# A chain of eight layers on one core: other instruction kinds on VectorE, closing rows in one instruction, routing in nine items, one maximum per causal head

## The chip, the core and the metric

The kernel runs on one core of a Trainium2 chip, as one program. The metric is the device time of one execution in microseconds. The kernel before takes 3289.19 us, the median of three runs (3284.95 to 3290.69).

## The reference

The input x is 16 x 256 x 256 (16 items of 256 tokens, 256 channels), with a context of the same shape and a mask of 16 x 256. Eight layers follow one another, each a residual addition:

```python
x = x + xattn0(layernorm(x), ctx)          # 16 heads, relu on q, k, v
x = x + ffn0(layernorm(x))                 # 8 experts, the best one
x = x + xattn1(layernorm(x), ctx, mask)    # 16 heads, own norms, masked
x = x + ffn1(layernorm(x))                 # 4 experts with low-rank parts
x = x + xattn2(layernorm(x), ctx)          # 16 heads, biases
x = x + block(layernorm(x))                # x + causal attention(norm(x)), then x + moe(norm(x))
x = x + xattn3(layernorm(x), ctx)          # 8 heads of 64
x = x + fp8_linear(layernorm(x))           # x and weight rounded to fp8, rows @ weight.T
```

The mixture in `block` keeps two of eight experts for each token: the logits are compared, the two largest chosen, and their outputs weighted. `fp8_linear` scales by 448 / max|x|, rounds to float8 and multiplies back.

## The kernel before, in words

The activations stay in SBUF as 32 tiles of 128 tokens. `attention()` is built for each attention layer; the unit of its work is one item of 256 tokens. It is software-pipelined: a list written out by hand (`slots()`, line 375 on, and `plan()`, lines 457 to 510) gives each period 16 slots. A period is one item in the steady state. In each slot TensorE does a head's scores and a head's product, and VectorE, ScalarE and GpSimd run the same list, each taking the entries that are its own. `SHIFT` says which item a step of a period is for: "l" is six items behind. Two attentions (the one that uses the context, a2, and the causal one, a3) run in one block, without a barrier; tiles of both are called a2... in the trace. Every step waits for semaphores counted by `Signal.at`.

What the change touches:

- **Biases and variances.** VBB (line 1154) is V's bias, spread over 128 rows: a tensor_scalar of ones by a column, twice, on VectorE. VE (lines 1284 to 1288) is the variance plus epsilon, made on VectorE; GpSimd raises it to the power -0.5 (line 734), with a constant tile `neghalf` of 8 columns.
- **GpSimd at the head of an attention.** It makes the normalised rows of item 0, then `keys()` and `others()` (lines 720 to 726) clear KS, QS, NM and VA; in the masked attention the mask rows MKF and MROW follow (lines 821, 822), which K needs. Then it issues the DMAs that move Q (line 598) and goes on to the next item. K is moved by SyncE's queue.
- **The maximum of a causal head** (line 1214). Scores of 256 queries against keys lie in one bank: 128 columns for the first 128 queries (which see only the first 128 keys), 256 for the second 128. Two VectorE reduces make the two maxima. TensorE then transposes the maxima of all heads (`maxT`).
- **The router** (class `Router`, line 72). Items are routed in five groups, `GROUPS = [(0, 4), (4, 8), (8, 12), (12, 14), (14, 16)]`. Items 0 to 13 have their logits made inside the causal attention, items 14 and 15 in the block of the routed experts. For a group VectorE ranks the experts of each token (`choose`, line 219), copies the running ranks that TensorE sums (`ranks`, `ranked`), works out which slots of 256 rows belong to which expert (`runs`, line 259) and each token's places (`places`, line 284). These are four items of the plan, in slots 1, 3, 5 and 7 of the period after the group's last logits. GpSimd then scatters each item's normalised rows into `slots` with four indirect DMAs (`scatter`, line 304), one item per period (`late`, line 317).
- **The entry of the routed experts** (`routed`, line 1939). Behind the barrier VectorE does the statistics of the last two items, their logits, the last group's routing, the table of slots, and the lower halves of the weights in 16 pieces (`low`, line 2131; ScalarE's `high`, line 2085, makes the upper ones). The pieces pass through a ring of four buffers, f2WF: piece j is loaded when low(j-4) is done. TensorE begins when the last low is done and the rows of the first slot are loaded, which waits for all scatters.
- **The quantised layer** (`quantised_linear`, line 2220). For each of eight units VectorE rounds (lines 2293 to 2301; the last is a subtraction of two SBUF tiles into Q), and writes the rows of an earlier unit from PSUM with scale and bias in four pieces of 256 columns (line 2315); GpSimd adds X and the result leaves (line 2259).

## Time and profile before

| | |
|---|---|
| median of three runs | 3289.19 us |
| the profiled execution | 3291.92 us, its span 3290.2 us |
| mean granted TensorE clock | 0.928 of full speed |
| TensorE busy | 2804.8 us (85%) |
| VectorE busy | 1978.9 us (60%) |
| ScalarE busy | 1666.2 us (51%) |
| GpSimd busy | 1142.0 us (35%) |
| causal attention with routing, from its first output to its last | 2045.1 to 2342.6 us |
| entry of the routed experts | 2343 to 2412 us |

Times are of one execution taken by the hardware profiler. A row of a timeline reads: start, duration, engine, line, operation, output and inputs with the number of instructions, and in brackets how long the engine had stood idle and what ended that. PE is TensorE, DVE VectorE, ACT ScalarE, POOL GpSimd, SP SyncE; the letter q behind a name means its queue of DMA issues. A view by windows gives the busy time of each engine in a stretch, the granted clock (PEclk) and the DMA traffic. Several instructions that overlap in one row, as x2 or x4, share one duration from the first start to the last end.

### The profile page before, as it was taken

Reading aid. Unit: us, or ns where it says so; the run is one execution under the profiler, and the core shown is the slowest. Engines: PE = TensorE matmul, PEld = TensorE weight load, DVE = VectorE, ACT = ScalarE, POOL = GpSimd, SP = SyncE. Lnnn points to the kernel's source line nnn. Section 1 sums busy time; section 2 is a strip of 40 time slices with the busy share of each in tenths; the row PEclk is TensorE's granted clock in tenths of the full one; section 3 lists DMA queues with packets and bytes.
Section 4 is the critical chain, followed back from the end, with each engine's and each line's share of the span. In section 5 each row is a group of like instructions: output and inputs, shape, how many; then the busy total and the mean of one; then the engine's idle time right before and its main releaser. Section 6 shows DMA issues by size and latency. Waiting matters only on the chain. (4 is left out here: it accounts for less than half of the span.)

```text
span 3290.2 us, 69997 instructions
## 1 busy us (share of the span) xinstructions
PE 2804.8 (85%) x26085; PEld 1887.7 (57%) x26085; DVE 1978.9 (60%) x4610; ACT 1666.2 (51%) x3073; POOL 1142.0 (35%) x1192
## 2 busy tenths in 40 slices
PE   4998685888789999999969999988469959999993
PEld 2554453555346666666645556666258846666672
DVE  4887556888555344443358887788554344555547
ACT  2778332777544444444437776666455523333332
POOL 6653008777000000000043334465410074555423
PEclk8999896999889999999979999999789978999995
DMA  3332002221214000000011211111243243332301
GB/s 116 79 75 56 14 8 88 67 67 64 45 55 151 1 1 1 1 1 1 1 60 59 75 48 48 43 56 63 80 145 92 88 114 71 79 87 61 76 21 51
DMA packets 164743, 189.87 MB, mean 58 GB/s; under 512 B 25968, under 2 KB 136832, under 8 KB 164256
## 3 DMA queue, kind: packets, MB, share of 16 engines
q1 hardware_dynamic: 147520, 143.44, 14.8%
q0 software_dynamic: 16896, 41.97, 4.9%
q8 instruction: 218, 3.57, 0.5%
q14 instruction: 109, 0.89, 0.1%
HBM read 67.09 MB, written 41.42 MB: 33 GB/s over the span
## 5 line engine op out<-in xcount | busy, mean ns | idle before, releaser
L1920 DVE TENSOR_TENSOR f1H<-f1HF,f1H 128x512 bf16<-128x512 f32 x256 | 176.6, 692 | 398.2 <-ACT f1H L1760 398.2
L1693 PE MATMUL ps<-f1xT,f1w 128*128 128x512 bf16 x1536 | 378.3, 383 | 6.1 <-ACT f1H L1760 6.1
L1715 PE MATMUL ps<-f1w,f1H 128*128 128x256 bf16 x3072 | 378.1, 273 | 0.0
L1715 PEld LDWEIGHTS ps<-f1w,f1H 128*128 128x128 bf16 x3072 | 301.4, 98 | 90.2 <-issue 1.1
L1757 ACT ACTIVATE f1HF<-ps 128x512 f32<-128x512 f32 x256 | 152.8, 597 | 333.9 <-PE ps L1693 333.8
L1075 ACT ACTIVATE a2PT<-ps 128x512 f32<-128x512 f32 (+1 forms) x512 | 260.1, 542 | 81.5 <-PE ps L892 58.1
L1693 PEld LDWEIGHTS ps<-f1xT,f1w 128*128 128x128 bf16 x1536 | 148.2, 98 | 150.8 <-issue 16.7
L869 PE MATMUL ps<-a2KS,a2QS 49*128 49x256 bf16 (+1 forms) x1024 | 173.7, 263 | 56.1 <-DVE a2NM L1217 19.7
L734 POOL TENSOR_TENSOR a2RS<-a2VE,neghalf 128x4 f32<-128x4 f32 x32 | 32.7, 1021 | 539.7 <-DVE a2VE L1288 539.7
L1603 POOL TENSOR_TENSOR f1RS<-f1VE,neghalf 128x4 f32<-128x4 f32 x8 | 8.1, 1011 | 574.6 <-DVE f1VE L1903 574.6
L1217 DVE TENSOR_REDUCE a1NM<-ps 128x2 f32<-128x512 f32 x256 | 165.7, 686 | 38.6 <-PE ps L869 37.3
L1217 DVE TENSOR_REDUCE a0NM<-ps 128x2 f32<-128x512 f32 x256 | 165.2, 685 | 35.1 <-PE ps L869 34.7
L1217 DVE TENSOR_REDUCE a2NM<-ps 128x2 f32<-128x512 f32 x256 | 165.6, 685 | 25.1 <-PE ps L869 23.1
L1075 ACT ACTIVATE a4PT<-ps 128x512 f32<-128x512 f32 x128 | 76.0, 597 | 193.7 <-PE ps L881 193.7
L881 PE MATMUL ps<-a2QS,a2KS 51*128 51x256 bf16 (+1 forms) x1024 | 171.0, 262 | 0.2 <-ACT a2PT L1075 0.2
L1214 DVE TENSOR_REDUCE a2NM<-ps 128x1 f32<-128x128 f32 (+1 forms) x512 | 150.2, 349 | 28.9 <-PE ps L892 26.9
L1075 ACT ACTIVATE a1PT<-ps 128x512 f32<-128x512 f32 x256 | 143.0, 595 | 26.6 <-PE ps L881 24.7
L809 POOL DMA_INDIRECT Y<-results,IX x64 | 63.3, 990 | 260.7 <-DMA results<-f2OB 243.7
L869 PEld LDWEIGHTS ps<-a2KS,a2QS 49*128 49x128 bf16 x1024 | 66.8, 94 | 148.4 <-DVE a2NM L1217 50.6
L1760 ACT ACTIVATE f1H<-ps 128x512 bf16<-128x512 f32 x256 | 151.7, 593 | 0.0
L1075 ACT ACTIVATE a0PT<-ps 128x512 f32<-128x512 f32 x256 | 141.5, 593 | 15.5 <-PE ps L881 12.0
L869 PE MATMUL ps<-a4KS,a4QS 128*128 128x256 bf16 (+1 forms) x512 | 126.6, 283 | 16.6 <-issue 8.6
(533 smaller groups left out, 7043.0 us busy)
## 6 DMA issues: line engine op xcount, KB each, us to landing
a2KS<-a2KH SPq DMA_DIRECT2D x192, 64.0 KB
a2QS<-a2QH SPq DMA_DIRECT2D x192, 64.0 KB
a4KS<-a4KH SPq DMA_DIRECT2D x96, 128.0 KB
a4QS<-a4QH POOLq DMA_DIRECT2D x96, 128.0 KB, 4.2
slots<-zeros SPq DMA_DIRECT2D x1, 9984.0 KB, 31.9
f2XG<-slots SPq DMA_DIRECT2D x39, 256.0 KB, 3.0
results<-f2OB SPq DMA_DIRECT2D x39, 256.0 KB, 2.1
f1WF<-in_f_w SPq DMA_DIRECT2D x32, 256.0 KB, 2.7
```

The lines of the kernel that those rows point to most:

```text
L734: nc.gpsimd.tensor_tensor(RS[:, h], VE[:, h], g["neghalf"][:, 0:4], ALU.pow).then_inc(S["rstd_ready"].sem, 1)
L809: nc.gpsimd.indirect_dma_start(GB[:, t % 4, k, :], None, g["results"][:, :], bass.IndirectOffsetOnAxis(ap=g["IX"][:, k, t:t + 1], axis=0)) ...
L869: m = nc.tensor.matmul(bank[:, at:at + keys], QS[r0:r1, u % RING, ch, gi, t * P:t * P + P], KS[r0:r1, u % RING, ch, gi, 0:keys], start=(ch ...
L881: m = nc.tensor.matmul(bank[:, at:at + SEQ - q0], KS[r0:r1, u % RING, ch, gi, t * P:t * P + P], QS[r0:r1, u % RING, ch, gi, q0:SEQ], start ...
L1075: nc.scalar.activation(PT[:, ic % 8, 0:n_], ps[:, 2 + (uc * NH + ic) % 3, 0:n_], ACT.Exp, scale=scale).then_inc(S["p_ready"].sem, 1)
L1214: s_ = nc.vector.tensor_reduce(NM[:, u % 2, t, col:col + 1], bank[:, lo:hi], AX.X, MAX, negate=True)
L1217: s_ = nc.vector.tensor_reduce(NM[:, u % 2, :, col:col + 1], bank.rearrange("p (t k) -> p t k", t=2), AX.X, MAX, negate=True)
L1693: m = nc.tensor.matmul(ps[:, (u * NCH + i) % 2, :], w1[:, x, kt, i * P:i * P + P], xT[:, half, y, kt, :], start=(j == 0), stop=(j == len(t ...
L1715: m = nc.tensor.matmul(out, H[:, (u * NCH + i) % HR, x, t * P:t * P + P], w2[:, y, i, :], start=first, stop=(f == YC - 1 and j == 2 and no ...
L1757: nc.scalar.activation(HF[:, (u * NCH + i) % 2, :], ps[:, (u * NCH + i) % 2, :], cfg["gelu"], **bias).then_inc(S["h_full"].sem, 1)
L1760: nc.scalar.activation(H[:, (u * NCH + i) % HR, 0, :], ps[:, (u * NCH + i) % 2, :], cfg["gelu"], **bias).then_inc(S["h_hi"].sem, 1)
L1920: nc.vector.tensor_tensor(H[:, (u * NCH + i) % HR, 1, :], HF[:, (u * NCH + i) % 2, :], H[:, (u * NCH + i) % HR, 0, :], SUB).then_inc(S["h_ ...
```

## The change

It has six parts.

1. VBB, VE, and the last subtraction of Q and WQ in the quantised layer become scalar_tensor_tensor; epsilon comes from columns 4 to 7 of `neghalf`, which VectorE sets at the start. In the masked attention `keys()` and `others()` run behind the mask rows.
2. The closing rows of a unit of the quantised layer are one scalar_tensor_tensor of 128x1024 instead of four of 128x256.
3. A causal head has one reduce over three blocks of 128 columns; behind the last head of an item a minimum (maxima are stored negated) joins the second and the third, and TensorE's transposes wait for that (`m_full`).
4. Routing is nine items, in slots 1 to 9; the group (8, 12) has its scatters two items to a period, behind slot 10.
5. The group (12, 14) is routed in the block of the routed experts (`PLACED = 3`), beside the statistics of the last two items, and all its scatters are issued there.
6. In that block lows 0 to 5 are spread between the routing steps, the table comes behind low 5, and ScalarE's highs and copies alternate.

```diff
+PLACED = 3
 def late(u):
-    a, b = [q for q in GROUPS if q[0] <= u < q[1]][0]
-    return BATCH + b - 1 + 6 + u - a
+    n, (a, b) = [(k, q) for k, q in enumerate(GROUPS) if q[0] <= u < q[1]][0]
+    return BATCH + b - 1 + 6 + (u - a) // (2 if n + 1 == PLACED else 1) if n < PLACED else None
...
-            put(1, "r_choose", "l", 0)
-            put(3, "r_rank", "l", 0)
-            put(5, "r_runs", "l", 0)
-            put(7, "r_places", "l", 0)
+            for k, n in enumerate(("r_compare", "r_select", "r_count", "r_rank", "r_need", "r_first", "r_jump", "r_place",
+                                   "r_index")):
+                put(1 + k, n, "l", 0)
...
-                        if r == "l" and v + 1 != GROUPS[n][1]:
+                        if r == "l" and (v + 1 != GROUPS[n][1] or n >= PLACED):
...
-                if router and k == 9:
+                if router and k == 10:
                     made += [("r_scatter", v, 0, None, None) for v in range(INSIDE) if late(v) == period]
...
-        NM = sb("NM", [P, 2, 2, P], F32)
+        NM = sb("NM", [P, 2, 3 if any(q.causal for q in stages) else 2, P], F32)
...
-                        nc.gpsimd.memset(g[n][:], v).then_inc(built.sem, 1)
+                        nc.gpsimd.memset(g[n][:, 0:4] if n == "neghalf" else g[n][:], v).then_inc(built.sem, 1)
...
-                        if u == 0 and not gather:
+                        if u == 0 and not gather and not mask:
                             keys()
                             others()
...
                                            ALU.is_equal, MUL).then_inc(S["mask_row"].sem, 1)
+                        if u == 0:
+                            keys()
+                            others()
...
-                        pe.wait_ge(S["s_max"].sem, S["s_max"].at(u, NH))
+                        if stage(u).causal:
+                            pe.wait_ge(S["m_full"].sem, S["m_full"].at(u % BATCH, 1))
+                        else:
+                            pe.wait_ge(S["s_max"].sem, S["s_max"].at(u, NH))
...
-                        v = nc.vector.tensor_scalar(VBB[:, kt, :], g["onesf"][:, 0:P], VB[:, kt:kt + 1], None, MUL)
+                        v = nc.vector.scalar_tensor_tensor(VBB[:, kt, :], g["onesf"][:, 0:P], VB[:, kt:kt + 1],
+                                                           g["onesf"][:, 0:P], MUL, MUL)
...
                         if stage(u).causal:
-                            for t, (lo, hi) in enumerate(((0, P), (P, P + SEQ))):
-                                s_ = nc.vector.tensor_reduce(NM[:, u % 2, t, col:col + 1], bank[:, lo:hi],
-                                                             AX.X, MAX, negate=True)
+                            s_ = nc.vector.tensor_reduce(NM[:, u % 2, :, col:col + 1],
+                                                         bank[:, 0:3 * P].rearrange("p (b k) -> p b k", b=3),
+                                                         AX.X, MAX, negate=True)
...
+                        if stage(u).causal and i == NH - 1:
+
+                            dve.wait_ge(S["s_max"].sem, S["s_max"].at(u, NH))
+                            nc.vector.tensor_tensor(NM[:, u % 2, 1, 0:NH], NM[:, u % 2, 1, 0:NH], NM[:, u % 2, 2, 0:NH], MIN
+                                                    ).then_inc(S["m_full"].sem, 1)
...
-                        a1, b1 = (1.0 + EPS, EPS * EPS) if stage(u).ln == 2 else (1.0, EPS)
-                        s_ = nc.vector.tensor_scalar(VE[:, h, 0:2], v, a1, b1, MUL, ADD)
+                        a1, b1 = (1.0 + EPS, 6) if stage(u).ln == 2 else (1.0, 4)
+                        s_ = nc.vector.scalar_tensor_tensor(VE[:, h, 0:2], v, a1, g["neghalf"][:, b1:b1 + 2], MUL, ADD)
...
+                router.ranks(pe, PLACED, ps[:, 4, :])
                 for u in LATE:
                     router.transposes(pe, u, ps[:, u % 2, :])
...
-                for j in range(4):
-                    high(j)
-                for u in LATE:
-                    router.copied(act, u, ps[:, u % 2, :])
+                high(0)
+                high(1)
+                router.copied(act, INSIDE, ps[:, INSIDE % 2, :])
+                high(2)
+                high(3)
+                router.copied(act, INSIDE + 1, ps[:, (INSIDE + 1) % 2, :])
...
-                for u in LATE:
-                    router.stats(dve, u)
-                    router.negate(dve, u)
-                for u in LATE:
-                    router.kept(dve, u, ps[:, 2 + u % 2, :])
-                router.choose(dve, LAST)
+                router.stats(dve, INSIDE)
+                router.compare(dve, PLACED)
+                router.negate(dve, INSIDE)
+                router.stats(dve, INSIDE + 1)
+                router.select(dve, PLACED)
+                router.count(dve, PLACED)
+                router.negate(dve, INSIDE + 1)
+                router.ranked(dve, PLACED, ps[:, 4, :])
+                router.need(dve, PLACED)
+                router.first(dve, PLACED)
+                router.jump(dve, PLACED)
+                router.place(dve, PLACED)
+                router.index(dve, PLACED)
                 low(0)
+                router.kept(dve, INSIDE, ps[:, 2 + INSIDE % 2, :])
+                low(1)
+                router.kept(dve, INSIDE + 1, ps[:, 2 + (INSIDE + 1) % 2, :])
+                router.compare(dve, LAST)
+                router.select(dve, LAST)
+                router.count(dve, LAST)
+                low(2)
                 router.ranked(dve, LAST, ps[:, 5, :])
-                router.runs(dve, LAST)
-                router.places(dve, LAST)
+                router.need(dve, LAST)
+                router.first(dve, LAST)
+                router.jump(dve, LAST)
+                low(3)
+                router.place(dve, LAST)
+                router.index(dve, LAST)
+                low(4)
+                low(5)
                 table()
-                for j in range(1, len(PIECES)):
+                for j in range(6, len(PIECES)):
                     low(j)
...
-                    nc.vector.tensor_tensor(Q[:], t1, t2, SUB).then_inc(S["q_ready"].sem, 1)
+                    nc.vector.scalar_tensor_tensor(Q[:], t1, 1.0, t2, MUL, SUB).then_inc(S["q_ready"].sem, 1)
...
-                    for t in range(UT):
-                        acc = ps[:, 2 * (c % 2) + t // 2, (t % 2) * D:(t % 2) * D + D]
-                        v = nc.vector.scalar_tensor_tensor(OB[:, c % 2, t * D:t * D + D], acc, IS[:, 2:3], q8["BI"][:], MUL, ADD)
-                    v.then_inc(S["q_ob"].sem, 1)
+                    acc = ps[:, 2 * (c % 2):2 * (c % 2) + 2, :].rearrange("p b (t d) -> p (b t) d", d=D)
+                    bias = q8["BI"][:].rearrange("p (one d) -> p one d", one=1).to_broadcast([P, UT, D])
+                    nc.vector.scalar_tensor_tensor(OB[:, c % 2].rearrange("p (t d) -> p t d", d=D), acc, IS[:, 2:3], bias,
+                                                   MUL, ADD).then_inc(S["q_ob"].sem, 1)
...
+                nc.vector.memset(g["neghalf"][:, 4:6], EPS)
+                nc.vector.memset(g["neghalf"][:, 6:8], EPS * EPS)
```

The new functions `compare`, `select` and `count` hold the instructions of `choose`, `need`, `first` and `jump` those of `runs`, `place` and `index` those of `places`; no instruction is added or taken away by that.

## Rows read from the trace of the kernel before

**Rows 1.** Windows: us; PE, PEld, DVE, ACT, POOL busy; PEclk; DMA share; GB/s.

```profile
523.90:557.00 33.10, 15.22 (x96) 8.02 (x96) 16.98 (x44) 4.25 (x7) 31.78 (x36) 0.67 0.30 73
2144.57:2171.34 26.77, 20.98 (x294) 14.30 (x290) 24.00 (x86) 14.44 (x29) 15.92 (x14) 0.94 0.15 51
2171.34:2191.07 19.73, 18.89 (x288) 13.60 (x284) 15.48 (x57) 14.03 (x29) 14.06 (x14) 1.00 0.22 71
2230.60:2257.10 26.50, 19.99 (x298) 13.78 (x295) 24.04 (x87) 14.44 (x29) 15.90 (x14) 1.00 0.15 51
2343.00:2412.00 69.00, 4.03 (x53) 2.90 (x53) 36.79 (x97) 21.31 (x22) 33.17 (x31) 0.50 0.51 178
```

**Rows 2.** timeline of VectorE at the heads of three attentions: start us, us, instruction.

```profile
505.67 12.23 DVE L1154 TENSOR_SCALAR a1VBB<-onesf,a1VB 128x128 f32<-128x128 f32 x2
...
1667.00 0.88 DVE L1171 SCALAR_TENSOR_TENSOR a2wq<-a2PT,a2VEC,a2wq 128x256 bf16<-128x256 f32 x2 [6.41 <-ACT a2wq L1056]
...
1671.72 5.38 DVE L1154 TENSOR_SCALAR a2VBB<-onesf,a2VB 128x128 f32<-128x128 f32 x2
...
2672.74 4.72 DVE L1284 TENSOR_SCALAR a4VE<-a4MV 128x2 f32<-128x2 f32 x1
```

**Rows 3.** timeline of GpSimd at the heads of the first two of these.

```profile
506.95 3.51 POOL L721 MEMSET a1KS<- 128x4096 f32 x1
...
519.07 1.06 POOL L822 TENSOR_SCALAR a1MROW<-a1MKI 8x256 bf16<-8x256 int32 x1
524.03 3.14 POOL L598 DMA_DIRECT2D a1QS<-a1QH  x6 [3.90 <-issue]
...
1666.08 3.51 POOL L721 MEMSET a2KS<- 128x4096 f32 x1
```

**Rows 4.** quantised layer: timelines of VectorE and GpSimd, and line 2301 by itself.

```profile
3239.65 3.02 DVE L2301 TENSOR_TENSOR q8Q<-q8T 128x1024 bf16<-128x1024 f32 x1
3242.60 1.65 DVE L2315 SCALAR_TENSOR_TENSOR q8OB<-ps,q8IS,q8BI 128x256 bf16<-128x256 f32 x4
...
3238.50 3.09 POOL L2259 TENSOR_TENSOR q8OUT<-X,q8OB 128x1024 f32<-128x1024 f32 x1 [20.36 <-DVE q8T L2296]
...
L2301 DVE TENSOR_TENSOR q8Q<-q8T x8: 1225/3024/3025, 3227.6 to 3275.7; 128x1024 bf16<-128x1024 f32 x8
```

**Rows 5.** timeline of VectorE and GpSimd in a routing period of the causal attention.

```profile
2320.80 1.13 DVE L276 SCALAR_TENSOR_TENSOR f2FREE<-f2T 128x8 f32<-128x8 f32 x1
...
2320.74 1.17 POOL L177 TENSOR_TENSOR f2XS<-a2WF,f2XS 128x512 bf16<-128x512 f32 x1
```

**Rows 6.** causal maxima, line 1214, in one unit by form, and in a row of four.

```profile
L1214 DVE TENSOR_REDUCE a2NM<-ps 128x1 f32<-128x256 f32 x16 | 6.6, 414 | 0.0
L1214 DVE TENSOR_REDUCE a2NM<-ps 128x1 f32<-128x128 f32 x16 | 4.5, 283 | 0.8 <-PE ps L892 0.8
...
2154.49 1.14 DVE L1214 TENSOR_REDUCE a2NM<-ps 128x1 f32<-128x128 f32 x4
```

**Rows 7.** TensorE's waits in five periods (2045 to 2144), then in the first routing period.

```profile
PE ps L869 <- DVE a2NM L1214: 3.6, 6, 1.6
...
PE ps L869 <- DVE a2NM L1214: 3.2, 3, 1.8
PE ps L242 <- DVE f2SEL L233: 1.7, 1, 1.7
```

**Rows 8.** timeline of GpSimd around the entry of the routed experts.

```profile
2325.18 1.05 POOL L313 DMA_INDIRECT slots<-f2XS,IX  x1 [3.27 <-DVE IX L302]
...
2360.06 0.14 POOL L2009 IOTA f2JI<- 128x1 int32 x1 [4.25 <-POOLq L601]
```

**Rows 9.** timeline of VectorE and TensorE in the entry of the routed experts.

```profile
2377.02 1.28 DVE L2136 SCALAR_TENSOR_TENSOR f2w<-f2WF,f2GA,f2w 128x1024 bf16<-128x1024 f32 x1
...
2390.93 1.28 DVE L2136 SCALAR_TENSOR_TENSOR f2w<-f2WF,f2GA,f2w 128x1024 bf16<-128x1024 f32 x1 [1.38 <-ACT f2w L2089]
...
2412.29 1.86 PE L2042 MATMUL ps<-identb,f2XG 128*128 128x128 bf16 x16 [27.75 <-issue]
```

112 lines of the change are left out of this document (69 added, 43 removed).

## The prediction

> **What bounds the kernel now.** I went from the time by stage to the two engines' timelines in the stages that the edits touch. TensorE carries most stages, but not everywhere: in the causal attention a plain period of 19.73 us holds 18.89 us of TensorE work and 15.48 of VectorE, so TensorE paces it, with 0.84 us left over. The two periods that route a whole group of four items last 26.77 and 26.50 us, with VectorE busy for 24.00 and 24.04 and TensorE for 20.98 and 19.99: there VectorE paces [rows 1]. From 2343 to 2412 us TensorE works 4.03 of 69 us [rows 1]: that is the routed experts' entry, a chain of routing, scatters and weight preparation. At the head of the masked attention (523.9 to 557 us) it works 15.22 of 33.10 us, with GpSimd busy for 31.78; there, and in the closing quantised layer, the waits of VectorE and GpSimd count at full price.
>
> **1. Another instruction kind.** VectorE's tensor_scalar of 128x128 into VBB, twice, lasts 12.23 us in the masked attention and 5.38 in the next one, and the tiny VE in the gathering attention 4.72; each ends with a series of GpSimd memsets [rows 2, 3]. Its scalar_tensor_tensor of two SBUF inputs at 1667.00 takes 0.88 for the pair under the memset that runs from 1666.08 to 1669.59 [rows 2, 3]: that kind is not held by a memset. So VBB ends at some 507.3 (a GpSimd operation that reads runs until 507.0, then 0.3), and the held time goes. What is late next: GpSimd's own queue. Before, its keys' and others' memsets run from 506.95 to 517.92 and the mask rows to 520.13, then it waits 3.90 for the Q move at 524.03, for VectorE's late Q and K [rows 3]. After, the mask rows come first (to 509.2), K and Q are ready under the memsets, which end at 520.3, and the Q move follows at once. From that move to 557 GpSimd is busy for 31.78 of 33.10 us [rows 1], so it takes along what it gains: **-3.8**, of at most 6.3 that the K side gets (the mask rows come 11 earlier, but K's move must wait for the memset of KS); 0 if the K side or the mask load becomes last. In the next attention VBB's release brings K's lower half forward by about **-1.3** (0 to -4). In the gathering attention the power that follows VE stands on GpSimd behind the very memsets that hold VE [rows 2], and GpSimd's gathers and Q move come after it, so the freed time has no taker: **0** (to -2). The two new memsets of the constants, 0.1 each, run before anything waits: 0.
>
> **The quantised layer's subtraction** is the doubtful one. As tensor_tensor it takes 1.23 us at its shortest and 3.02 in the median; the one at 3239.65 stands beside GpSimd's addition, which reads SBUF from 3238.50 to 3241.59, and six of the eight are held so [rows 4]. As scalar_tensor_tensor it has the same two inputs in SBUF. The nearest row of that kind beside a GpSimd operation that reads is the one at 2320.80: 1.13 instead of 0.16, until GpSimd's addition of 1.17 ends [rows 5]. So it is held alike: **0**; the other bound is that it isn't held, 6 x 1.79 = -10.8. The Trainium skill ("SBUF — State Buffer", Who interferes with whom) has a rule that speaks against this edit: a VectorE instruction with two SBUF inputs contends with a GpSimd instruction that reads SBUF, and not with one that only writes. By that rule the edit on Q brings nothing and that on VBB all; rows 5 and the pair at 1667.00 agree.
>
> **2. Closing rows.** Four pieces take 1.65 us, one 128x1024 operation 1.23 [rows 4]: 0.42 less, at seven of eight units on VectorE's chain: **-3.0**. The bounds are 0 (GpSimd, which starts on the rows, may move its hold along) and -4. The quantised weights' single operation, 0.7 us, keeps its length: 0.
>
> **3. One maximum per causal head.** Before, 16 reduces of 128x128 (0.28) and 16 of 128x256 (0.41), 11.1 us a unit. They overlap: two pairs last 1.14, a pair 0.57 [rows 6]. From 0.28 for 128 and 0.41 for 256 elements, 384 take 0.55, spaced 0.48: 16 x 0.09 = 1.4 less, against which the minimum of 128x16 and its own wait add 0.3 to 0.6 at the end of the unit: VectorE gets 0.8 to 1.1 back. TensorE's transposes of the maxima now wait for that minimum; it is behind the last reduce by 0.3 and they are a slot away: 0. The wider memset of NM adds 0.3 in the head of the stage, beside VectorE's work: 0. TensorE waits 3.6 us on these reduces in the first five periods [rows 7], 0.7 in each. I take 0.35 for each of eleven plain periods: **-4**, between 0 and -8 (nearly all of the 0.84).
>
> **4. Nine routing items, two scatters to a period.** A routing period needs 24.0 us of VectorE, 23.2 with part 3, and lasts 26.6: 2.5 us of it are holes where four long items stand in front of a reduce for which TensorE waits. With pieces of 1 to 2 us in nine slots I halve the holes: 24.8, **-1.8** twice, and -1.2 for the group of half the size: -4.8 (0 to -9; nothing if the links between items, now with TensorE's ranks in slot 4 and waits in more places, make new holes). The two scatter items of a period issue eight indirect DMAs instead of four, 10.1 us of GpSimd's queue at 1.265 each. Behind them stand the power, and through it VectorE's negate and ScalarE's normalising of the last items; they come some 4 us later, in periods whose own work ends on TensorE, and GpSimd's chain below counts them.
>
> **5. The entry of the routed experts.** Before: the last attention's output at 2342.6, the group (12, 14) routed behind it until 2350.8, four scatters until 2355.8, then 4.25 us to the next block's first GpSimd instruction at T0 = 2360.06; low(0) at T0 + 17, the last low a little before TensorE, TensorE at T0 + 52.2, after 27.75 us without work [rows 8, 9]. After: that group is routed inside the block beside the statistics, the power and the split, which leave VectorE idle for most of the first 12 us of the block. T0 is set by GpSimd: from the index of group (8, 12) at about 2325, two items' scatters (10.1), power, normalising and split (4), two items' again (10.1), and 4.25 behind them, T0 = 2353.9: -6. low(0), which frees the ring of four weight buffers, comes at T0 + 11.5 behind the routing of group 3, and the lows follow the weights' loads as before: another -5.8. Together **-11.8**. Bounds: -4 (only the block starts sooner, by less; all 16 scatters of the last four items stand in the block as before, and the lows are paced by loads) and -16.
>
> Sum: -3.8 - 1.3 - 3.0 - 4.0 - 4.8 - 11.8 = **-28.7**. The profiled execution took 3291.92 us, 2.7 above the median of the runs; 3291.92 - 28.7 = 3263.2, and on the median 3289.19 - 28.7 = **3260.5 us**.
>
> **The rivals.** (A) The subtraction isn't held in the new kind: 10.8 more, 3249.7. For it: under a memset the kind matters, as the pair at 1667.00 beside VBB shows, so it might beside a reader too; against it, the one row of that kind beside a reader [rows 5]. Chance 0.17. (B) The causal stage stays with TensorE, whose 18.89 of 19.73 leaves little, and the entry is paced by the weights' loads: parts 3 and 4 give 2 and part 5 gives 6: -16, 3273. For it: at 2390.93 a low waits for ScalarE's high of the same piece, as most of those behind it [rows 9]. Chance 0.22. (C) The instruction kind does nothing for VBB, since two operands make it wait as before: the 5.1 of part 1 go, 3265.6; the pair at 1667.00 is against it. Chance 0.08. (D) Slower: the clock. In the first routing period, where TensorE waits 3.2 us on the maxima and 1.7 on the selection [rows 7], the granted clock is 0.94 and its work 20.98 us instead of 19.99: the drop cost 1.0 [rows 1]. If nine items, with their waits in every slot of VectorE, spread such holes over the period, TensorE could stay at the lower of its two levels: its 19 us would be 38. From two whole periods this decides: -28.7 + 38 = +9, 3298. Against it: the second routing period has its holes at 1.00. Chance 0.03. The forecast has 0.50.
>
> **The numbers.** A measurement of this kernel tells about 0.2%, 6.6 us, from no change. All cases but D lie below 3282.6; B with low ends in every part could come near it. The range reaches from A with some gain less than full (3247) to a little below B (3274). Faster 0.93, same 0.04, slower 0.03.
>
> **What would show it.** VBB pairs of under 1.5 us; the first Q move of the masked attention at about 520.3; the subtraction still 3.02 in six of eight; closing rows as one of about 1.2; plain causal periods of 19.4 and routing periods near 25; T0 six us sooner against the last attention's output, and 46 instead of 52 us from T0 to TensorE's first turn. I am wrong if the subtraction falls to 1.2, if routing periods stay at 26, or if the lows wait for loads so that T0 + 52 stands.

## The result and the profile after

The changed kernel takes 3273.39 us, median of six runs (3270.53 to 3276.84), where the kernel before took 3289.94 beside it. The ratio is 0.9951, with a 95% interval from 0.9935 to 0.9967: 16 us faster (11 to 21), more than the 0.2% that a measurement tells from no change. The profiled execution took 3275.65 us, its span is 3273.9 us, at a mean clock of 0.928. Another chip gave 0.9954 (0.9940 to 0.9967). One execution of a later kernel (the old order of memsets) took 11164.78 us at a granted clock of 0.239 and is left out of its ratio.

The forecast was 28.7 us. To see where the rest went, I cut both traces at VectorE's write of each unit's output (line 1360 before, 1404 after) and at the landmarks of the prediction. All figures are of the two profiled executions:

| stretch | forecast | before | after | difference |
|---|---|---|---|---|
| masked attention: first power to first Q move | -3.8 | 28.44 | 24.39 | -4.05 |
| next attention: first power to first scores | -1.3 | 26.88 | 25.25 | -1.63 |
| causal stage: twelve plain periods | -4 | 231.89 | 228.24 | -3.65 |
| causal stage: two full routing periods | -3.6 | 53.27 | 57.82 | **+4.55** |
| third last output to T0 (third routing, tail, block change) | -7.2 | 48.19 | 43.52 | -4.67 |
| T0 to TensorE's first expert turn | -5.8 | 52.23 | 46.64 | -5.59 |
| quantised layer: last output to the end | -3.0 | 77.33 | 74.69 | -2.64 |

Five of the seven are within 1 us of what was said. Two aren't: the routing periods are 8.2 us off, with the wrong sign, and the stretch to T0 is 2.5 off. That is nearly the whole difference of 12 us between forecast and measurement. The entry of the routed experts and the block change hold parts 5 and 6 of the change together; no run takes them apart.

What these rows leave out (layers that the change doesn't touch, and the gathering attention) moves by several us between executions of one kernel: from the first expert turn to the first output of the gathering attention the changed kernel took 370.44 us in one profile and 363.68 in another, and its executions on the second chip reach from 3261.31 to 3280.18 us. So below I compare stretches, and use whole times for the verdicts only. Periods of the causal stage repeat to 0.2 us, but where TensorE's clock falls they can be 1 to 1.6 us apart.

Windows over the first routing period, a plain one, the second and the third routing period, and the entry, after; they answer to [rows 1], with the same columns:

```profile
2136.91:2165.72 28.81, 21.09 (x295) 14.63 (x293) 23.20 (x71) 14.34 (x29) 15.61 (x14) 0.94 0.14 48
2165.72:2185.25 19.53, 18.83 (x285) 13.57 (x283) 14.66 (x41) 14.07 (x29) 14.06 (x14) 1.00 0.22 71
2224.34:2253.35 29.01, 21.69 (x295) 14.75 (x293) 23.17 (x72) 14.33 (x29) 15.53 (x14) 0.88 0.14 48
2307.68:2330.68 23.00, 18.55 (x185) 11.04 (x184) 12.66 (x45) 11.54 (x25) 9.07 (x10) 0.70 0.12 41
2343.80:2398.00 54.20, 4.22 (x55) 3.09 (x56) 37.95 (x97) 21.19 (x22) 29.97 (x27) 0.54 0.64 217
```

VectorE has less to do than before (23.20 instead of 24.00 us), and yet the period is 2 us longer. The clock is lower in the second and the third: TensorE's same work takes 21.69 instead of 19.99 us, and in the third 18.55 instead of 14.46 (the clock was 0.90 there before). In the first it is 0.94 as before, with 21.09 us of work for 20.98.

The timeline of VectorE and GpSimd at the heads of the two attentions, after, to [rows 2, 3]:

```profile
508.05 1.62 DVE L1182 SCALAR_TENSOR_TENSOR a1VBB<-onesf,a1VB 128x128 f32<-128x128 f32 x2
514.58 0.88 DVE L1343 SCALAR_TENSOR_TENSOR a1KF<-ps,a1bk,a1MKF 128x256 f32<-128x256 f32 x2 [4.91 <-PE ps L884]
...
1668.12 0.61 DVE L1182 SCALAR_TENSOR_TENSOR a2VBB<-onesf,a2VB 128x128 f32<-128x128 f32 x2
...
1666.25 3.51 POOL L746 MEMSET a2QS<- 128x4096 f32 x1
...
510.76 1.06 POOL L844 TENSOR_SCALAR a1MROW<-a1MKI 8x256 bf16<-8x256 int32 x1
519.14 3.50 POOL L748 MEMSET a1VA<- 128x4096 f32 x1
522.60 3.14 POOL L620 DMA_DIRECT2D a1QS<-a1QH  x6
```

VBB is short (its second piece stands beside GpSimd's subtraction, so the pair takes 1.62 and not 0.61 us), the mask rows end at 511.8, and the Q move starts with no idle time, right behind the memset. In the span's own time it is 1.4 us sooner; from the first power, at 498.21 here and at 495.59 before, it is 4.05 sooner. The first output of this attention comes 99.85 us behind the power instead of 103.32, so 3.5 us of it are still there then. In the next attention the first scores come 1.63 us sooner and the first output 0.64 (83.03 instead of 83.67).

The quantised layer, after, to [rows 4]:

```profile
3225.64 3.02 DVE L2369 SCALAR_TENSOR_TENSOR q8Q<-q8T 128x1024 bf16<-128x1024 f32 x1
3228.59 1.27 DVE L2383 SCALAR_TENSOR_TENSOR q8OB<-ps,q8IS,q8BI 128x1024 bf16<-128x1024 f32 x1
...
3224.49 3.09 POOL L2327 TENSOR_TENSOR q8OUT<-X,q8OB 128x1024 f32<-128x1024 f32 x1 [19.99 <-DVE q8T L2364]
...
L2369 DVE SCALAR_TENSOR_TENSOR q8Q<-q8T x8: 1224/3024/3026, 3214.0 to 3259.8; 128x1024 bf16<-128x1024 f32 x8
```

The subtraction is as long as it was, in six of eight units. The closing rows are one operation of 1.27 us.

The selection of the first full group, in the timelines of VectorE and TensorE, and TensorE's waits in that period, after, to [rows 7]:

```profile
2138.49 0.67 DVE L227 TENSOR_TENSOR a2WF<-f2G 128x512 f32<-128x512 f32 x1
2145.83 0.64 DVE L242 TENSOR_SCALAR f2SEL<-f2RK 128x64 bf16<-128x64 f32 x1
...
2146.62 0.21 PE L252 MATMUL ps<-f2SEL,prior 128*128 128x64 bf16 x1 [5.11 <-DVE f2SEL L242]
...
PE ps L252 <- DVE f2SEL L242: 5.1, 1, 5.1
PE ps L894 <- DVE a2NM L1252: 2.2, 3, 1.0
```

This is what the prediction did not have in it. VectorE begins to compare at 2138.49 and has the selection at 2146.47, because it takes the three items in three slots, with two reduces, K's lower half, a unit's product and its statistics between them: 8 us, where one item took 4.1. TensorE is at its rank product in slot 4 by 2141.5 and waits 5.11 us. Before, the item was in one piece in slot 1, the ranks in slot 3, and the wait was 1.7.

The entry of the routed experts, after, to [rows 8, 9]:

```profile
2351.20 0.14 POOL L2055 IOTA f2JI<- 128x1 int32 x1 [4.25 <-POOLq L623]
...
2343.80 0.69 DVE L1404 TENSOR_TENSOR Y<-ps,Y 128x512 f32<-128x512 f32 x1 [1.53 <-PE ps L884]
2363.14 1.28 DVE L2184 SCALAR_TENSOR_TENSOR f2w<-f2WF,f2GA,f2w 128x1024 bf16<-128x1024 f32 x1
...
2397.83 1.86 PE L2088 MATMUL ps<-identb,f2XG 128*128 128x128 bf16 x16 [18.69 <-issue]
```

T0 is 2351.20, low(0) at T0 + 11.9, TensorE at T0 + 46.6, as forecast (11.5 and 46). T0 comes 7.40 us behind the last output instead of 17.51.

What sets T0 is in GpSimd's timeline, after; the first and the last row each open a series of eight indirect DMAs, four for each of two items:

```profile
2321.24 1.05 POOL L336 DMA_INDIRECT slots<-f2XS,IX  x1 [7.00 <-DVE IX L325]
...
2335.03 0.61 POOL L176 CAST f2XS<-a2WF 128x512 bf16<-128x512 f32 x1 [3.14 <-ACT a2WF L166]
...
2337.04 1.05 POOL L336 DMA_INDIRECT slots<-f2XS,IX  x1 [0.17 <-issue]
```

The first scatter starts 13.56 us behind the third last output (13.31 before). Eight scatters take 9.9 us, the power, the wait for ScalarE's normalising and the split 5.9, eight more scatters 9.9, and then come the 4.25 us: 43.5 in all.

And the clock around the second wait and behind the third, in windows of the changed kernel, columns as in [rows 1]:

```profile
2229.00:2234.30 5.30, 0.24 (x7) 0.28 (x8) 5.13 (x13) 1.46 (x3) 5.15 (x6) 0.78 0.16 52
2234.30:2237.00 2.70, 2.70 (x25) 1.88 (x23) 0.87 (x3) 0.49 (x1) 1.27 (x2) 0.50 0.19 55
2237.00:2240.00 3.00, 3.00 (x39) 1.64 (x38) 1.20 (x5) 1.31 (x3) 0.00 (x0) 0.70 0.00 0
...
2318.00:2323.00 5.00, 5.00 (x44) 2.86 (x40) 2.54 (x14) 3.21 (x8) 1.46 (x2) 0.50 0.03 12
2323.00:2328.00 5.00, 5.00 (x40) 2.89 (x40) 1.21 (x3) 2.64 (x5) 3.78 (x5) 0.55 0.29 103
```

TensorE works 0.24 of 5.3 us while it waits, and the clock falls to half within that wait; then it runs at 1.2 GHz for 2.7 us and for a part of the next three. The third wait, of 4.4 us, ends at 2315.2, and TensorE stays at 1.2 GHz until about 2327.5, though it works all the time from 2318 on.

### The profile page after: what moved, and what is told of

Same layout as the page of the kernel before. It is cut to its first block and busy times, and to the rows that moved or that the text cites. A ratio compares the mean times of both kernels' runs of the same rounds, so it can differ in the third digit from the quotient of the medians.

```text
span 3273.9 us, 69748 instructions
## 1 busy us (share of the span) xinstructions
PE 2807.5 (86%) x26085; PEld 1890.0 (58%) x26085; DVE 1943.4 (59%) x4348; ACT 1666.0 (51%) x3073; POOL 1142.5 (35%) x1192
## 5 line engine op out<-in xcount | busy, mean ns | idle before, releaser
L1252 DVE TENSOR_REDUCE a2NM<-ps 128x3 f32<-128x384 f32 x256 | 134.5, 553 | 32.8 <-PE ps L917 30.0
```

What stands on the lines that cost most here:

```text
L1252: s_ = nc.vector.tensor_reduce(NM[:, u % 2, :, col:col + 1], bank[:, 0:3 * P].rearrange("p (b k) -> p b k", b=3), AX.X, MAX, negate=True)
```

## The experiments

All edits are made to the changed kernel, the last ones on top of the ranks in slot 6. Ratios are to the kernel before on the same chip. The four kernels with two reduces, the old kinds, the old order and the later addition have ratios whose intervals overlap that of the changed kernel (0.9935 to 0.9967): what is said of them rests on stretches of one profile each.

### Four items again; and nine, with the ranks two slots later

```diff
-            for k, n in enumerate(("r_compare", "r_select", "r_count", "r_rank", "r_need", "r_first", "r_jump", "r_place",
-                                   "r_index")):
-                put(1 + k, n, "l", 0)
+            for k, n in ((1, "r_compare"), (1, "r_select"), (1, "r_count"), (3, "r_rank"), (5, "r_need"), (5, "r_first"),
+                         (5, "r_jump"), (7, "r_place"), (7, "r_index")):
+                put(k, n, "l", 0)
```

> The changed kernel with the routing's nine functions called in four items again, in slots 1, 3, 5 and 7, all else as changed. Theory W (TensorE's rank product in slot 4 waits for a selection that now lies behind three slots of VectorE's work, 5.1 and 4.4 us instead of 1.7 and 2.7, and its clock falls after the wait): the two full routing periods go from 28.8 and 29.0 us to 25.5 to 26.5, the third from 23.0 to 17 to 18.5, the wait on the selection falls under 2.8 us, and the kernel to about 3264 us (3261 to 3268). Rival X (the one maximum and its minimum make the stage slow): periods stay at 28.5 to 29, the time at 3273. Rival Y (two scatters a period delay the tail): the full periods recover, the third stays at 22 to 23, the time is about 3268.5.

Ratio 0.9917 (0.9902 to 0.9931), 3270.82 us. Windows over the two full routing periods and the last period, then the wait on the selection in the second:

```profile
2139.50:2166.97 27.47, 22.54 (x295) 15.46 (x293) 23.71 (x71) 14.32 (x29) 16.05 (x14) 0.88 0.15 50
2225.60:2253.98 28.38, 23.62 (x295) 16.26 (x293) 23.71 (x71) 14.49 (x29) 15.97 (x14) 0.82 0.14 48
2326.47:2344.63 18.16, 11.71 (x120) 7.29 (x119) 2.90 (x8) 6.74 (x14) 13.45 (x15) 0.73 0.23 80
...
PE ps L252 <- DVE f2SEL L242: 1.7, 1, 1.7
```

The wait on the selection is back at 1.7, and the full periods are 27.47 and 28.38 us: shorter than with nine items in slots 1 to 9, but outside what I had said, and longer than before the change (26.78 and 26.49). The clock did that: TensorE is busy for 22.54 and 23.62 us with work that takes 20 at full clock. These periods differ from those of before mainly in the one maximum per head, and the waits are no longer than they were. Whether the one maximum lowers the clock or this execution fell further by chance, one profile can't tell; by the two executions named below chance is good for 1 to 1.6 us of a period.

The third period is 18.09 us, from 23.00, but the last one went from 13.12 to 18.16, so their sum is the same. That is theory Y (two scatters a period delay the tail) in another place: see the split scatters below.

```diff
+            for k, n in ((1, "r_compare"), (2, "r_select"), (3, "r_count"), (6, "r_rank"), (7, "r_need"), (8, "r_first"),
+                         (9, "r_jump"), (10, "r_place"), (11, "r_index")):
+                put(k, n, "l", 0)
...
-                if router and k == 10:
+                if router and k == 12:
```

> The changed kernel with nine items, but the ranks two slots later: compare, select and count in slots 1 to 3, ranks in slot 6, the rest in 7 to 11, scatters behind slot 12. Theory W: TensorE waits under 0.7 us for the selection, the full routing periods take 23.5 to 25.5 us, the third 16.5 to 18, and the kernel 3260 us (3257 to 3266). If it is the number of items itself, with a wait in every slot, that costs (rival Z), the full periods stay above 27.5 us and the time at 3270 or more. By Y the third period stays at 22 to 23.

Ratio 0.9917 (0.9901 to 0.9932), 3268.43 us. Windows over the two full routing periods:

```profile
2139.77:2164.22 24.45, 19.83 (x295) 13.74 (x293) 22.68 (x71) 14.64 (x29) 13.89 (x12) 1.00 0.14 46
2223.22:2249.21 25.99, 21.52 (x296) 14.74 (x295) 22.74 (x71) 14.86 (x29) 14.31 (x13) 0.93 0.14 46
```

They take 24.45 and 25.99 us, 4.36 and 3.02 less than in the changed kernel, with the same number of items. The second is a little above what I had said, and so is the third (18.45 us), which keeps a wait of 3.2 us on the selection. From the two full periods that wait is gone; 4.1 us of waits on the maxima remain, in five pieces of at most 1.7, and the clock is 1.00 and 0.93. So the number of items doesn't cost (rival Z falls), it is the distance between selection and ranks. Against the kernel before it is -2.33 and -0.50, where the prediction had -1.8 each: the argument on the holes was right, for another schedule than the one that was built. The sum of the last two periods is 36.2 us again. From the last output ahead of the causal stage to T0 it took 322.24 us, with four items 326.10, in the changed kernel 329.58; as whole kernels nine items with late ranks and four items can't be told apart (both 0.9917).

### Two reduces per causal head again

```diff
-                            s_ = nc.vector.tensor_reduce(NM[:, u % 2, :, col:col + 1],
-                                                         bank[:, 0:3 * P].rearrange("p (b k) -> p b k", b=3),
-                                                         AX.X, MAX, negate=True)
+                            for t, (lo, hi) in enumerate(((0, P), (P, P + SEQ))):
+                                s_ = nc.vector.tensor_reduce(NM[:, u % 2, t, col:col + 1], bank[:, lo:hi],
+                                                             AX.X, MAX, negate=True)
```

> The changed kernel with two reduces per causal head again, no minimum, and the transposes waiting for the reduces. If one maximum gives what the plain periods show (19.55 instead of 19.75 us, and one of 19.5 instead of 21.1), it is slower than the changed kernel by 2 to 6 us: 3275 to 3279. By rival X it is faster, 3265 to 3270. Routing periods get 0.5 to 1.5 us longer by the first, shorter by the second.

Ratio 0.9957 (0.9943 to 0.9971), 3281.62 us. The plain periods are 19.72 us, to the hundredth those of before, and the one of 21.09 is 20.91 instead of 19.47. The full routing periods are 30.82 and 29.46 us. From the last output of the attention ahead of it to its own last output the stage took 325.92 us, 3.7 more than in the changed kernel. One maximum per head is worth having: 0.17 to 0.33 us in most plain periods, 1.6 in one, 3.65 over twelve. Not everywhere: the third routing period is 21.14 us with two reduces, at a clock of 0.76, where the changed kernel has 23.00 at 0.70. From the last output ahead of the stage to T0 the two reduces cost 4.05 us (333.63 instead of 329.58), so rival X falls.

### The kind of VBB and VE, and the order of memsets and mask rows

```diff
-                        v = nc.vector.scalar_tensor_tensor(VBB[:, kt, :], g["onesf"][:, 0:P], VB[:, kt:kt + 1],
-                                                           g["onesf"][:, 0:P], MUL, MUL)
+                        v = nc.vector.tensor_scalar(VBB[:, kt, :], g["onesf"][:, 0:P], VB[:, kt:kt + 1], None, MUL)
...
-                        s_ = nc.vector.scalar_tensor_tensor(VE[:, h, 0:2], v, a1, g["neghalf"][:, b1:b1 + 2], MUL, ADD)
+                        s_ = nc.vector.tensor_scalar(VE[:, h, 0:2], v, a1, b1, MUL, ADD)
```

> The changed kernel with VBB and VE as tensor_scalar again; the order of memsets and mask rows stays changed. If the kind is what freed VBB, the pair in the masked attention is held from 508 until GpSimd's series of memsets ends at about 522.6 (over 10 us instead of 1.62), the Q move comes 4 to 8 us later than 522.6, and the time is 3277 to 3283. If the order alone did it, VBB ends by 512 and the time stays at 3273 to 3275. In the next attention VBB takes about 5.4 us, worth 0.7.

Ratio 0.9941 (0.9921 to 0.9962), 3280.38 us, by its ratio no slower than the changed kernel. The heads of the masked attention, VectorE and GpSimd:

```profile
507.50 0.83 DVE L1182 TENSOR_SCALAR a1VBB<-onesf,a1VB 128x128 f32<-128x128 f32 x2
...
508.34 1.15 POOL L787 TENSOR_TENSOR a1CS<-a1CN,a1CS 128x512 bf16<-128x512 f32 x1
522.57 3.14 POOL L620 DMA_DIRECT2D a1QS<-a1QH  x6
```

Not what I expected of either case, and for a reason that makes this run undecided here. With the old kind VBB took 0.83 us, and the Q move is at 522.57. But its two pieces were done at 508.33, 0.01 us before GpSimd's subtraction started (508.34) and with it a series of GpSimd instructions without a gap. Before the change, VBB began at 505.67 and that subtraction at 505.86, in front of VBB's second piece, which then was held to the end of the series. Which of the two happens is a matter of 0.2 us. So the run shows that the new order and a short VBB give the gain, whatever the kind, and not that the old kind would always be short. In the next attention the kind is worth what was said: VBB takes 5.62 us with the old kind instead of 0.61, and from the first power to the first scores 27.09 us instead of 25.25 (25.2 to 26.1 in all kernels with the new kind). The gathering attention takes 39.27 us from its first power to its first scores with the old kind and 39.20 with the new (39.41 before): nothing, as forecast.

The other half, the new kinds with the old order:

```diff
-                        if u == 0 and not gather and not mask:
+                        if u == 0 and not gather:
                             keys()
                             others()
...
-                        if u == 0:
-                            keys()
-                            others()
```

> The changed kernel with the memsets ahead of the mask rows again, the kinds of VBB and VE as changed. With tensor_scalar and the new order VBB took 0.83 us, so the order alone would do: then this kernel has a short VBB (under 2 us) and yet the mask rows at about 522.6, K behind them, Q behind K, and the Q move 3 to 4 us later than in the changed kernel: from unit 0's output on 3.4 us later, about 3277. If the kind gives the gain by itself, the Q move stays within 1 us and the time at 3273.

Ratio 0.9962 (0.9949 to 0.9974), 3277.53 us. VectorE and GpSimd at the head of the masked attention:

```profile
507.91 0.61 DVE L1179 SCALAR_TENSOR_TENSOR a1VBB<-onesf,a1VB 128x128 f32<-128x128 f32 x2
523.44 0.88 DVE L1340 SCALAR_TENSOR_TENSOR a1KF<-ps,a1bk,a1MKF 128x256 f32<-128x256 f32 x2 [14.91 <-issue]
...
522.29 1.06 POOL L844 TENSOR_SCALAR a1MROW<-a1MKI 8x256 bf16<-8x256 int32 x1
527.25 3.14 POOL L620 DMA_DIRECT2D a1QS<-a1QH  x6 [3.90 <-issue]
```

VBB takes 0.61 us, and VectorE then stands idle until the mask rows are there (KF at 523.44, behind MROW, which ends at 523.35). GpSimd waits 3.90 us for the Q move, to the hundredth as long as before the change [rows 3]. The hold of 12.23 us, the longest in the trace, lay beside a wait for the mask rows: without the new order its removal doesn't bring the Q move forward at all. What that costs the attention is less clear. Its first output comes 101.85 us behind the first power (99.85 in the changed kernel, 103.32 before), 2.0 us later and not the 3.4 that I had said; with the new order it comes at 97.4 to 100.3. The last one comes at 381.58, against 382.24 in the changed kernel and 388.04 before, and from 378.0 to 384.9 in all kernels with the new order: at the end of the stage one profile doesn't tell the two orders apart.

### GpSimd's addition behind the subtraction

```diff
-                        pool.wait_ge(S["q_step"].sem, S["q_step"].at(n + 2, 2))
+                        pool.wait_ge(S["q_ready"].sem, S["q_ready"].at(n + 2, 1))
```

> The changed kernel; GpSimd's addition of a unit in the quantised layer waits for the subtraction two units on, not for the step before it, so that the two don't meet. The hold is then gone (the subtraction 1.23 us in all eight), and the addition falls on the closing rows, which read one SBUF tile and PSUM, and on the tensor_scalars behind them. If rows from PSUM aren't held, and the tensor_scalar is held for what is left (0.9 us), a unit takes 5.9 instead of 6.84 us and the layer 5 to 6 us less: 0.9935 of the kernel before. If the addition holds the closing rows too, the unit stays at 6.8 and the time with it.

Ratio 0.9943 (0.9929 to 0.9957), 3271.37 us. A unit in the timelines of VectorE and GpSimd:

```profile
3225.83 1.22 DVE L2369 SCALAR_TENSOR_TENSOR q8Q<-q8T 128x1024 bf16<-128x1024 f32 x1
3226.97 1.28 DVE L2383 SCALAR_TENSOR_TENSOR q8OB<-ps,q8IS,q8BI 128x1024 bf16<-128x1024 f32 x1
3228.17 1.70 DVE L2361 TENSOR_SCALAR q8T<-q8T 128x1024 int32<-128x1024 int32 x1
...
3227.20 2.12 POOL L2327 TENSOR_TENSOR q8OUT<-X,q8OB 128x1024 f32<-128x1024 f32 x1 [22.50 <-DVE q8Q L2369]
```

The subtraction takes 1.22 us, the closing rows 1.28, though GpSimd's addition runs beside them, and the addition 2.12 instead of 3.10. The tensor_scalar behind them is held to 1.70, where it takes 0.68 alone. A unit lasts 6.06 us instead of 6.84, and the layer 68.94 instead of 74.69: -5.75, at the upper end of what was said. The whole kernel shows less of it: 3271.37 us, where the changed kernel took 3274.29 on the same chip, with intervals that overlap. The overlap was the cost of this layer, and it goes by moving one of the two, not by the kind.

### Item 9's scatters behind the power

In the last period TensorE waits for something that had not been on my list. Two rows of GpSimd, one of ScalarE, one more of GpSimd, and TensorE's longest wait in the last period of the kernel with ranks in slot 6:

```profile
2327.15 0.96 POOL L336 DMA_INDIRECT slots<-f2XS,IX  x1 [0.31 <-issue]
2328.13 0.73 POOL L152 TENSOR_TENSOR f2RS<-f2VE,neghalf 128x2 f32<-128x2 f32 x1
...
2329.09 1.09 ACT L166 ACTIVATE a2WF<-Y,f2NEG,f2RS 128x256 f32<-128x256 f32 x2 [3.86 <-DVE f2NEG L158]
...
2330.25 0.61 POOL L176 CAST f2XS<-a2WF 128x512 bf16<-128x512 f32 x1 [1.39 <-ACT a2WF L166]
...
PE ps L1041 <- ACT a2PT L1103: 5.7, 1, 5.7
```

GpSimd issues the eighth indirect DMA at 2327.15 and the power behind it at 2328.13; ScalarE's normalising needs that (through VectorE's negate) and stands idle for 3.86 us in front of the exponentials, and TensorE waits for those for 5.7 us. In the changed kernel itself that wait is 1.7 us, as before the change. The edit, on top of the ranks in slot 6:

```diff
                 if router and k == 12:
-                    made += [("r_scatter", v, 0, None, None) for v in range(INSIDE) if late(v) == period]
+                    made += [("r_scatter", v, 0, None, None) for v in range(INSIDE) if late(v) == period and v != 9]
+                if router and k == 2 and period == late(9) + 1:
+                    made.append(("r_scatter", 9, 0, None, None))
```

> The kernel with ranks in slot 6, and item 9's scatters moved from slot 12 of their period to slot 2 of the next, behind the power of the second last item's statistics. Theory: in the last two periods GpSimd's queue bounds (eight scatters, then the power, then ScalarE's normalising and its exponentials for which TensorE waits 5.7 us), and idles for 3 us during the normalising. With the power first, the last period takes 13 to 15 instead of 17.7 us, and the entry's first GpSimd instruction comes 3 to 4 us sooner: 3262 us against 3265.7 in the profile of the kernel with ranks in slot 6. If VectorE's or ScalarE's own chain bounds the tail, it stays at 3265.

Ratio 0.9918 (0.9904 to 0.9931), 3264.96 us. GpSimd's timeline:

```profile
2321.62 0.96 POOL L336 DMA_INDIRECT slots<-f2XS,IX  x1 [0.30 <-issue]
2322.61 0.73 POOL L152 TENSOR_TENSOR f2RS<-f2VE,neghalf 128x2 f32<-128x2 f32 x1
2323.52 1.04 POOL L336 DMA_INDIRECT slots<-f2XS,IX  x1 [0.19 <-issue]
2344.53 0.14 POOL L2057 IOTA f2JI<- 128x1 int32 x1 [4.25 <-POOLq L625]
```

The power is between the items now. The last period takes 14.23 us instead of 17.73, but the third 20.26 instead of 18.44, at a clock of 0.75 instead of 0.81, and T0 comes 1.4 us sooner against the third last output (41.5 us, from 42.9). I had said 3 to 4 us. GpSimd's queue sets T0, and in it only 1.39 us were idle behind the power; that is what the edit could take. The longer third period isn't the reason: in the next kernel it is 18.29 us, and T0 comes at 41.55.

### All three edits, one scatter item per period, and the changed kernel once more

> Ranks in slot 6, item 9's scatters behind the next period's power, and GpSimd's addition in the quantised layer behind the subtraction: the three edits that gained, together. If they add up (9.6 us from the causal stage to the entry, 5.8 in the quantised layer), it takes 15 us less than the changed kernel: 0.9905 of the kernel before, 0.988 to 0.993. The entry and the layer are far apart, so I expect no interaction.

Ratio 0.9865 (0.9843 to 0.9886). This chip ran the kernel before in 3342.08 us, 50 more than the others, and in my kernel's trace the plain causal periods behind the first routing took 24 to 26 us instead of 19.5, with waits of TensorE on its own issue (2.3 us) and on ScalarE (up to 4.3) that only the other trace from that chip has. I have no cause for that, and use the ratio for nothing. The same kernel on another chip:

> The kernel with all three edits once more, since in its first run the periods of the causal stage from the first routing on took 5 to 6 us more than in any run before, beside a kernel before that was 50 us slower too: that was the chip, not the edits. On a chip where the kernel before takes 3290 us: 3258 us, ratio 0.9905 (0.989 to 0.992), plain periods of 19.5, T0 to T0 + 47 as in the changed kernel, the quantised layer 68.95. If the ratio stays near 0.9865 with the kernel before at 3290, I have missed 12 us of gain.

Ratio 0.9893 (0.9878 to 0.9909), 3255.08 us beside 3292.74. The stretch from the last output ahead of the causal stage to T0 takes 320.46 us (329.58 in the changed kernel, 333.34 before) and the quantised layer 68.94. It beats both kernels, and was to reach 0.9905.

The other way out of the double scatters, in two runs, the first on the same odd chip:

```diff
-    return BATCH + b - 1 + 6 + (u - a) // (2 if n + 1 == PLACED else 1) if n < PLACED else None
+    return BATCH + b - 1 + 6 + u - a if n < PLACED and u < 11 else None
...
-                for u in range(GROUPS[PLACED][0], BATCH):
+                for u in range(GROUPS[PLACED][0] - 1, BATCH):
                     router.scatter(pool, u)
```

> The kernel with ranks in slot 6, but one item's scatters per period (8, 9, 10) and item 11's in the entry's block, so 20 indirect DMAs there instead of 16. Rival Y again: the last period is 12.8 instead of 17.7 us. If GpSimd's queue sets the block's start, the start comes about 10 us sooner after the third last output than with doubled scatters, and if the entry is paced by the lows, it takes the same 46.8 us: 3259. If the scatters pace the entry, it takes 3 to 5 us longer there, 3262; if they were the whole bound, nothing is gained: 3266.

Ratio 0.9885 (0.9865 to 0.9905), 3301.92 us beside 3342.08. From the third last output to T0 it took 40.12 us, where the other kernel on that chip took 45.55: 5.4 us less, not the 10 that I had said. From T0 to TensorE's first expert turn it took 47.55 instead of 46.86.

> Ranks in slot 6, one item's scatters per period with item 11's in the entry's block, and GpSimd's addition behind the subtraction. In the run before, the four more indirect DMAs in the block cost 0.7 us and the last period lost its 4.9 us of waiting. So from the third last output to TensorE's first expert turn it should take 2 to 4 us less than the kernel with item 9's scatters behind the power: 3255 us at 3290 for the kernel before, 0.9895. If GpSimd's queue in the block binds instead, it is the same or slower by up to 2 us.

Ratio 0.9893 (0.9877 to 0.9908), 3256.93 us. From the third last output to T0 it takes 38.51 us instead of 41.55 with the split, and from T0 to TensorE's first expert turn 46.95 instead of 46.64. Together that is 2.7 us less, of the 2 to 4 that I had said. But its first routing period, in which the two kernels are the same, was 26.05 us at a clock of 0.93, where the other had 24.48 at 1.00. As whole kernels the two can't be told apart.

> The changed kernel as it is, beside the next three on one chip: 0.995 of the kernel before, and in its trace the wait on the selection 5.1, 5.1 and 4.4 us again. What is open is whether the low clock in the routing periods (0.94, 0.88, 0.70) is the same in another execution; if it is chance, the three periods differ from 28.8, 29.0 and 23.0 us by over 1 us.

Ratio 0.9954 (0.9940 to 0.9967), 3274.29 us. The three routing periods took 28.81, 29.00 and 23.01 us, against 28.81, 29.01 and 23.00 in the first trace, with granted clocks of 0.94, 0.88 and 0.70 in both. So the fall isn't chance, it comes with the schedule. How long it lasts can differ: in the kernel with the addition behind the subtraction, whose causal stage is the same, the second period took 30.05 us at 0.83, and in the one with the old kinds 30.30 at 0.83.

## Why the prediction was right, and where not

The direction was right and 3273.39 lies inside the range, 0.6 us from its end. The forecast itself was 13 us too low. That the time lies inside is in part luck: the upper end, 3274, was taken from rival B's 3273, which came about otherwise, and one of the seven terms came out with the wrong sign.

- **Another kind of instruction: right in size, half wrong in reason.** The prediction let the change of kind free VBB and the order pass the gain on. In the masked attention the kind alone doesn't move the Q move, since K and Q wait for the mask rows; the order gives its 4 us, as long as VBB isn't held, and against that the kind is at best an insurance. By the first output 3.5 us are left of it. In the next attention (-1.63 for -1.3 at the first scores, -0.64 at the first output) and in the gathering one (0) it was right. Rival C is out: VBB took 0.61 us under a memset.
- **The subtraction: right.** It is held as a scalar_tensor_tensor just as it was, 3.02 us in six of eight, as the row at 2320.80 [rows 5] had it. Rival A is out. The rule of the Trainium skill ("SBUF — State Buffer", Who interferes with whom), that a VectorE instruction with two SBUF inputs contends with a GpSimd instruction that reads SBUF and not with one that only writes it, agrees with the trace: 3.02 us beside the addition, 0.61 for VBB under a memset.
- **Closing rows: right**, -2.64 for -3.0. One operation takes 1.27, not the 1.23 that I took from the subtraction; seven times 1.65 - 1.27 is 2.66. No run takes this part back, the sum alone speaks for it.
- **One maximum: right in sum**, -3.65 for -4 in the plain periods. But the 3.6 us of waits [rows 7] that I spread as 0.7 over each of five periods hold one wait of 1.6, and the period with 21.09 us gave 1.63 of the 3.65; none of the others gave more than 0.33. In the routing periods with nine items it gives 2.01 and 0.45 us more (30.82 and 29.46 without it).
- **Nine items: wrong**, +4.55 where I had -3.6. The failed step is "I halve the holes". (The 24.8 us are not quite that either: 23.2 and half of 2.5 are 24.45.) I looked at the holes in front of reduces and counted nothing for the selection, whose wait of 1.7 us stood in the same group of rows [rows 7] and went into rival D only. Three items in three slots take 8 us of VectorE's time until the selection is out, and the ranks in slot 4 are too near: 5.1 us. With the ranks in slot 6 the same nine items give -2.33 and -0.50.
- **The clock: priced, but in the wrong case.** Rival D had its mechanism at whole periods. It came in a smaller dose: behind the three waits TensorE ran at 1.2 GHz for 3, 4.5 and 12 us. Against the kernel before, whose clock fell a little too, its work is 0.1, 1.7 and 4.1 us longer (18.55 instead of 14.46 in the third). Rival D's argument against itself, that the second period has its holes at 1.00, held for waits of 1.8 us and not for one of 5.1.
- **Third routing and block change: -4.67 for -7.2.** GpSimd's queue sets T0 as was said; two terms of that chain were off. The third routing was to bring the scatters 1.2 us forward, and they start 13.56 us behind the third last output instead of 13.31. With four items again it is 13.55, so nine items and their wait aren't the reason, and none is shown. And "power, normalising and split (4)" take 5.9, because GpSimd stands idle for 3.14 us until ScalarE's normalising is done; with four items, and with ranks in slot 6, they take 4.15. The sentence that the late normalising falls "in periods whose own work ends on TensorE" did no harm here (the last period has 13.12 us, from 12.82), but it doesn't hold once the third period is short: then TensorE waits 4.8 to 5.7 us for the exponentials behind it.
- **The entry: right**, 46.6 us from T0 for 46. No run takes back the new order of the lows or the routing of group (12, 14) in this block, so which of them gave how much is not shown.
- **Rival B** gave 3273 too, by a causal stage that stays as it was and an entry that gives half. Neither happened: the entry gave all that was said, and the stage gained 3.65 in one place and lost 4.55 in another. Its time was met by accident.

**What stays open:** whether one maximum makes the clock fall further in the periods with four items, or that was one execution; how much the parts of the entry give one by one; how much of the 4 us of the Q move reaches the end of the masked attention; and what slowed the one chip.

## What to carry to other kernels

When an item of work is cut into pieces and spread over slots, look for who consumes its last result, and move the consumer by as many slots as the last piece has moved; otherwise a smoother engine makes the other one wait, and TensorE pays again in its clock. Before a hold is priced, ask what the held engine would wait for without it: removing the longest hold of this kernel (12.23 us) didn't bring the Q move forward by itself, since the mask rows came no sooner. Where two engines hold each other up at every unit, try to shift one of them beside an operation that isn't held, as the closing rows here, rather than change the instruction.

## What the runs showed of the hardware

- A scalar_tensor_tensor with two SBUF inputs is held by a GpSimd tensor_tensor (3.02 instead of 1.23 us), and not by a GpSimd memset: at 1668.12 the pair of VBB took 0.61 us under the memset of QS (1666.25 to 1669.76), where as tensor_scalar it took 5.38 and 5.62. With one of the two inputs in PSUM it isn't held by the tensor_tensor (1.28 us, as long as alone). A tensor_scalar of 128x1024 in SBUF is held by it (1.70 instead of 0.68 us).
- A wait of TensorE of 4.4 to 5.1 us was followed, each time, by a stretch at the lower clock, of very unequal length: 3, 4.5 and 12 us. Only in the third routing period did it cost nearly the wait's own length again (granted clock 0.70, 4.1 us more of the same work than before), and the next execution had the same. Waits of at most 1.8 us were followed by a fall in some periods (0.94 in the first routing period before, 0.93 with ranks in slot 6) and not in others (1.00), once in two executions of the same code.
